# Low halves of rotated queries and keys on GpSimd, with the rotated tile four deep and the sine product kept in the swapped tile

## What is computed

```python
q = q.reshape(b, t, H, DH).transpose(0, 2, 1, 3)
k = k.reshape(b, t, H, DH).transpose(0, 2, 1, 3)
...
q = cos * q + rotate_half(q) * sin
k = cos * k + rotate_half(k) * sin
scores = jnp.einsum('bhqd,bhkd->bhqk', q, k) / math.sqrt(DH)
causal = jnp.tril(jnp.ones((t, t), dtype=bool))
scores = jnp.where(causal, scores, -jnp.inf)
attn = jax.nn.softmax(scores, axis=-1)
```

## Time and profile before

| what | value |
|---|---|
| time before, median of 3 runs | 2292.76 us (2287.46 to 2299.47) |
| the profiled execution | 2291.23 us |
| its span in the profile | 2289.5 us |
| mean granted TensorE clock | 0.989 of full speed |
| PE busy | 2109.5 us (92%) |
| DVE busy | 1931.8 us (84%) |
| ACT busy | 1354.4 us (59%) |
| POOL busy | 1306.6 us (57%) |

### The profile page before, as it was taken

One profiled execution on the slowest core, in us unless ns is written; L12 is line 12 of the kernel. 1 busy time (PEld: TensorE's weight loads), 2 busy tenths in 40 slices (PEclk: granted clock), 3 DMA queues, 4 the chain that ended last, 5 costly groups with the idle time before them and its releaser, 6 DMA issues.

```text
span 2289.5 us, 52899 instructions
## 1 busy us (share of the span) xinstructions
PE 2109.5 (92%) x17682; PEld 1141.4 (50%) x17682; DVE 1931.8 (84%) x4485; ACT 1354.4 (59%) x2568; POOL 1306.6 (57%) x1462
## 2 busy tenths in 40 slices
PE   4999999889999999999999999999999888999999
PEld 2666666434444444444444444444444434666666
DVE  6777788788999899999989998999999865777776
ACT  3455444266667666666666676666666655445553
POOL 6666667454555455456545554554555425666664
PEclk9999999899999999999999999999999999999999
DMA  6656666444445444444444454444445423666665
GB/s 208 192 192 207 201 203 200 116 89 89 98 95 101 94 94 98 89 94 93 99 89 100 95 101 94 96 92 96 93 94 98 99 70 118 197 202 194 204 207 167
DMA packets 280391, 295.29 MB, mean 129 GB/s; under 512 B 45784, under 2 KB 263224, under 8 KB 280120
## 3 DMA queue, kind: packets, MB, share of 16 engines
q1 hardware_dynamic: 280120, 291.90, 50.3%
HBM read 140.08 MB, written 83.89 MB: 98 GB/s over the span
## 4 chain that ended last, share of the span: by engine, by line
PE 45%; DVE 33%; SPq 7%; issue 6%; DMA 5%; ACT 4%; DVEq 0%; ACTq 0%
PE bank L710 8%; DVE bank L996 7%; DVE at_mx L1006 7%; PE bank L728 7%; PE bank L1185 6%; PE bank L1202 6%; PE bank L1219 4%; PE bank L1280 4%; ACT probs L1073 3%; DVE turned L975 3%; DVE v_qk L981 3%; DVE turned L974 2%; DVE at_stats L107 2%; PE bank L1255 2%; PE bank L1167 2%
## 5 line engine op out<-in xcount | busy, mean ns | idle before, releaser
L1073 ACT ACTIVATE probs<-bank 128x512 f32<-128x512 f32 x1280 | 747.0, 603 | 456.9 <-PE bank L1185 447.5
L912 POOL TENSOR_SCALAR_AFFINE_SELECT probs<-probs 128x512 f32<-128x512 f32 x512 | 320.4, 638 | 661.1 <-ACT probs L1073 659.3
L1006 DVE TENSOR_REDUCE at_mx<-bank 128x1 f32<-128x384 f32 (+2 forms) x896 | 509.6, 608 | 78.5 <-PE bank L1167 77.0
L1185 PE MATMUL bank<-stacks 49*128 49x512 f16 (+3 forms) x2048 | 458.7, 302 | 71.4 <-ACT probs L1073 71.0
L996 DVE CUSTOM_DVE_ANT_0 bank<-bank,xn 128x512 f32<-128x512 f32 x512 | 351.6, 698 | 38.8 <-PE bank L1158 36.2
L1185 PEld LDWEIGHTS bank<-stacks 49*128 49x128 f16 x2048 | 136.0, 94 | 458.6 <-ACT probs L1073 334.2
L1162 PE MATMUL bank<-stacks 48*128 48x384 f16 (+2 forms) x1536 | 307.7, 275 | 22.1 <-DVE at_mx L1006 15.6
L1167 PE MATMUL bank<-mask,turn 64*128 64x128 bf16 (+2 forms) x896 | 230.7, 257 | 0.0
L1158 PE MATMUL bank<-stacks 48*128 48x512 f16 x512 | 198.5, 389 | 10.6 <-DVE at_mx L996 6.4
L924 POOL TENSOR_TENSOR turned<-turned 128x512 f32<-128x512 f32 x128 | 184.7, 1443 | 19.1 <-POOL turned L920 0.4
L628 ACT ACTIVATE turned<-bank,b1s 128x512 f32<-128x512 f32 x128 | 88.2, 689 | 181.0 <-PE bank L710 179.3
(11 more groups left out here) (145 smaller groups left out, 4619.6 us busy)
## 6 DMA issues: line engine op xcount, KB each, us to landing
stacks<-qk_image SPq DMA_DIRECT2D x384, 128.0 KB, 4.5
qk_image<-v_qk SPq DMA_DIRECT2D x128, 256.0 KB, 3.7
stacks<-w_hi SPq DMA_DIRECT2D x192, 128.0 KB, 3.7
stacks<-w_lo SPq DMA_DIRECT2D x192, 128.0 KB, 3.8
b2s<-in_b SPq DMA_DIRECT2D x128, 128.0 KB, 3.9
after_ffn<-probs SPq DMA_DIRECT2D x32, 512.0 KB, 6.5
at_x<-after_ffn SPq DMA_DIRECT2D x32, 512.0 KB, 4.1
late_x<-after_ffn SPq DMA_DIRECT2D x32, 512.0 KB, 4.7
```

The source lines that it names most:

```text
L912: nc.gpsimd.affine_select(out=ap, in_=ap, compare_op=ALU.is_ge, fill=0.0, base=0, pattern=[[0, d] for d in dims] + [[1, P]], channel_multi ...
L1006: nc.vector.tensor_reduce(o_ap, i_ap, AX_X, ALU.max).then_inc(max_done, 1)
L1073: nc.scalar.activation(probs[:, c, :], st_ps[c % 2][:], ACT.Exp, scale=DH ** -0.5).then_inc(exp_done, 1)
L1185: ins = nc.tensor.matmul(bank[:, col:col + T - q0], k_stack[ss.par][rows, j + ha, kt * P:(kt + 1) * P], q_stack[ss.par][rows, j + ha, q0:T ...
```

## The change

The low halves of queries and keys leave VectorE's list and come into GpSimd's. In slot 1 GpSimd makes low half 0 behind the rotation of tile 2, ahead of the masks 1 to 3, and low half 1 at the slot's very end, behind the rotation of tile 3. In slot 2 it makes low halves 2 and 3 behind the first mask and ahead of the normalisation of a later sample's input. The tile `rotated` gets four buffers, one per tile t, and the wait of the sum for earlier low halves goes from two tiles back to four. The room comes from `by_sin`: the sine product is written over `swapped`. The order on the other engines stays.

```diff
-        rope = [[self.turned[:, 2 * j + i, :] for i in range(2)] for j in range(4)]
+        rope = [self.turned[:, 0:2, :], self.turned[:, 2:4, :], self.turned[:, 4:8, :]]
...
-            nc.gpsimd.tensor_tensor(by_sin[t % 2][:], swapped[t % 2][:], sin_t[:], ALU.mult).then_inc(sin_done, 1)
-
-            wait(pool, qk_lo, idx - 1)
+            nc.gpsimd.tensor_tensor(swapped[:, t % 2, :], swapped[:, t % 2, :], sin_t[:], ALU.mult).then_inc(sin_done, 1)
+
+            wait(pool, qk_lo, idx - 3)
             pool.wait_ge(sin_done, idx + 1)
-            nc.gpsimd.tensor_tensor(rotated[t % 2][:], by_cos[t % 2][:], by_sin[t % 2][:], ALU.add).then_inc(rope_done, 1)
+            nc.gpsimd.tensor_tensor(rotated[:, t, :], by_cos[:, t % 2, :], swapped[:, t % 2, :], ALU.add).then_inc(rope_done, 1)
+
+        def rope_low(n, t):
+            pool.wait_ge(qk_hi, 4 * n.b + t + 1)
+
+            wait(pool, q_written if t < 2 else k_written, 32 * n.b)
+            nc.gpsimd.tensor_tensor(qk.lo[:, t, :], rotated[:, t, :], qk.hi[:, t, :], ALU.subtract).then_inc(qk_lo, 1)
...
             if g < 2 and sample(s + 1):
                 rope(s + 1, 2 * g)
+            if g == 1 and sample(s + 1):
+                rope_low(s + 1, 0)
+            if g == 2 and sample(s + 1):
+                rope_low(s + 1, 2)
+                rope_low(s + 1, 3)
             if g == 2 and sample(s + 2):
...
             if g < 2 and sample(s + 1):
                 rope(s + 1, 2 * g + 1)
+            if g == 1 and sample(s + 1):
+                rope_low(s + 1, 1)
...
-        def rope_low(n, t):
-            dve.wait_ge(qk_hi, 4 * n.b + t + 1)
-
-            wait(dve, q_written if t < 2 else k_written, 32 * n.b)
-            nc.vector.tensor_tensor(qk.lo[:, t, :], rotated[t % 2][:], qk.hi[:, t, :], ALU.subtract).then_inc(qk_lo, 1)
...
-                if g in (1, 2) and sample(s + 1) and n in (0, 3):
-                    rope_low(s + 1, 2 * (g - 1) + (n == 3))
```

More of the change, by code:

```diff
@@ L759, in attention @@
     cos_t, sin_t = sb("cos", [P, T], F32), sb("sin", [P, T], F32)
-    q_stack, k_stack, v, qk, (swapped, by_cos, by_sin, rotated), ones = mem.of_attention()
+    q_stack, k_stack, v, qk, (swapped, by_cos, rotated), ones = mem.of_attention()
     x = mem.at_x
@@ L973, in begin_rope @@
             wait(dve, rope_done, idx - 1)
-            nc.vector.tensor_tensor(by_cos[t % 2][:], x_ps[t % 2][:], cos_t[:], ALU.mult)
-            nc.vector.stream_shuffle(swapped[t % 2][:], x_ps[t % 2][:], [i ^ 1 for i in range(32)]).then_inc(rope_in, 1)
-        def rope_low(n, t):
-            dve.wait_ge(qk_hi, 4 * n.b + t + 1)
-            wait(dve, q_written if t < 2 else k_written, 32 * n.b)
-            nc.vector.tensor_tensor(qk.lo[:, t, :], rotated[t % 2][:], qk.hi[:, t, :], ALU.subtract).then_inc(qk_lo, 1)
+            nc.vector.tensor_tensor(by_cos[:, t % 2, :], x_ps[t % 2][:], cos_t[:], ALU.mult)
+            nc.vector.stream_shuffle(swapped[:, t % 2, :], x_ps[t % 2][:], [i ^ 1 for i in range(32)]).then_inc(rope_in, 1)
         def maxima(s, g, n):
@@ L1078, in rope_high @@
             wait(act, q_written if t < 2 else k_written, 32 * n.b)
-            nc.scalar.activation(qk.hi[:, t, :], rotated[t % 2][:], ACT.Copy).then_inc(qk_hi, 1)
+            nc.scalar.activation(qk.hi[:, t, :], rotated[:, t, :], ACT.Copy).then_inc(qk_hi, 1)
         def high_of(hi, n, c, ps_done, hi_done):
```

## The result

The changed kernel takes 2343.6 us (median of 4 runs, 2335.44 to 2344.82), the kernel before beside it 2290.49 us (4 runs). The ratio is 1.0218, with a 95% interval of 1.0179 to 1.0256: about 2% slower. The profiled execution of the changed kernel is the shortest of its four, 2335.44 us, with a span of 2333.7 us (2289.5 before) and a mean granted clock of 0.985; the other three had 0.980 to 0.983. The prediction was 2333, slower.

A forecast was written before the change was run, and what follows sets the result against it. PE and DVE were taken to bound the kernel by turns, PE close behind a full DVE. Late stacks make a sample 45.0 + 1.35 = 46.35 us; 31 x 1.35 = 42 us on 2291.2 gives 2333, range 2272 to 2364.

The forecast's parts named there:

- GpSimd's path: GpSimd, slots 1 and 2: from the first mask to low half 1's end 10.48 us, that end 9.2 us later.
- SP's path: SP's DMA queue: late query write, key write behind query reads, stacks ready at 1154.4, 1.3 us late for PE.
- The transposes: PE ahead of L1247: normalised input 0.3 us late, contained in the 1.3 us wait for the stacks.
- They can't meet: Low halves and rotations, all on GpSimd, no longer block each other at the shared ports; all rotations at 1.28 us.
- DVE's relief: Slots 1 and 2: a faster DVE brings PE 0.6 to 0.9 us a sample, 19 to 28 us in all.
- The rival "faster": DVE's relief comes through if GpSimd's low half takes about 0.8 us: 2263 to 2281 us, chance 0.17.

The follow-up runs named there:

- The square: Four kernels: query halves on VectorE or early on GpSimd, key halves on GpSimd ahead of or behind the normalisation; 45.42, 44.56, 44.69, 43.82 us a sample.
- the best kernel: Changed kernel with low halves 0 and 1 early in GpSimd's slot 1, 2 and 3 behind the normalisation: 2252.36 us, ratio 0.9828 to the kernel before.

## Why the prediction was right, and where it was not

- **GpSimd's path: right.** From the mask to the end of low half 1 it is 1109.28 - 1099.27 = 10.01 us, forecast 10.48. The low half takes 1.16 us, not 1.28, and two of them 2.27 instead of 2.60. So the low half lies just outside the 1.2 to 1.4 us beyond which the prediction called itself wrong, and the forecast held all the same. The rotations are short, as forecast: from 700 to 1700 us the product takes 1.27 us in the mean (1.40 before) and the sum 1.28 (1.45).
- **SP's path: right, in part by luck.** Query write to reads 2.99 us (forecast 2.95); query reads to key reads 9.48 (8.95); the reads of the keys at 1121.84, forecast 1146.1 - 24.3 = 1121.8; the stacks used at 1130.23, forecast 1130.1. That the end agrees to the tenth is luck: low half 1 ended 0.56 us earlier than forecast (1109.28 for 1134.14 - 24.3), and the key write held the reads 0.53 longer. The path itself gives 1154.4 - 1153.12 = 1.28 us a sample, the sum took 1.35, and 1.27 was measured. The mechanism is shown by the swap in SP's order. The Trainium skill's rule that each DMA engine takes a ring's descriptors in their order (DMA: Bandwidth & Descriptors, section Queues, rings and completion order) agrees with it: the key write takes 5.8 us to land behind the reads, 3.0 ahead of them.
- **The transposes: right in the sum.** 0.3 us late was forecast and 0.0 measured; the input was ready at 1115.75, forecast 1140.74 - 24.3 = 1116.4. It was called covered by the wait for the stacks, and the doubled low half 3 bears that out.
- **"They can't meet": wrong.** I took what holds for the low halves and rotations to hold for all of VectorE's work. DVE's other operations with two SBUF inputs stayed, and low half 1 came to lie on them. The Trainium skill's rule, which I had cited for the opposite (SBUF — State Buffer, section SBUF: two separate sides), says that the one that starts first holds the shared ports for its whole instruction. It names no size, and the trace agrees even with 128x4 elements: 0.16 us become 1.13, and the operation ends 0.02 us after GpSimd's. This stand of 0.93 us did not spoil the total, because the stacks' path ran beside it and was longer; the swap in SP's order, without that cover, was 0.7% slower than before where the other terms alone would have made it faster.
- **DVE's relief: mis-sized.** I had 0.39 us for slot 1 and 0.17 for slot 2 from PE's busy time, with 0.9 as the most in all. The square gives about 0.74 and 0.47, and the best kernel 1.21 together. PE's busy share counts modelled ends, which hide room: PE was called busy 10.08 of 11.00 us in a slot that it then ran in 10.25. The rival "faster" came out that way only after the halves were moved, not by a low half of 0.8 us.
- **The clock: left out.** 42 us were forecast and 44.2 found in the span. The 28 samples at full clock make 35.4 of them, 3.5 come from the one whose clock fell, and the other 5.3 mostly from the start, at a lowered clock. So the near agreement of the totals is partly luck too: 1.27 in each of 31 samples would be 39. The median of the four, 53 us over before, is farther off. A term for the clock is missing from the sum, whatever its size.

## What to carry over

When work moves to GpSimd, look at which VectorE operations with two SBUF inputs lie beside its new place, the tiny ones too, and put it where VectorE has none: the maxima, which read PSUM, kept their 0.7 us beside it. One input alone is no safe sign, as L115 and L117 show with low half 1 made twice. In a DMA queue that one engine feeds in order, ask for each write that somebody waits for what is queued ahead of it. The same move was 2.2% slower in one order and 1.7% faster in another: the place of an operation in an engine's list decided, not its cost.

## What the hardware showed that I had not expected

- A VectorE operation on 128x4 elements took 1.13 us instead of 0.16 while GpSimd ran a two-input operation, and 0.51 while it ran a mask, which has one input. With low half 1 made twice, L115 took 1.13 too, which reads one tile and constants. At 1018.39 it ended 0.03 us after GpSimd's second copy did. Whether it was held up for the same reason is open; the section of the Trainium skill named above also counts VectorE's two-port modes among what is blocked, and no run shows in which mode L115 ran.
- GpSimd's subtraction of an fp16 tile from an fp32 tile into fp16 took 1.16 us (1147 to 1195 ns, 84 times), against 1.28 for the same shape in fp32.
- A stand of PE of 1.43 us was followed by about ten microseconds at the 1.2 GHz level (granted 0.50), worth 3.2 us; a stand of 1.63 was followed by some three. But the length of the stand alone doesn't decide it: 1.69 us at 945.52 in the changed kernel, 1.97 at 1052.49 with only the query halves on GpSimd, and 1.87 at 1635.24 with low half 1 made twice were followed by a clock of 1.00. What else it hangs on, these runs don't say.
